# The convolution loop: a tile's matmuls are split around the next tile's last batch of transposes, and layer norm steps move behind the one-hot rows

## What is computed

```
x = x + deformable_conv(group_norm(x))        # 3 x 3 taps, learned offsets and masks
t = t + mamba_both_ways(layer_norm(t))        # two selective scans, forward and backward
t = t + graph_attention_moe(layer_norm(t))    # 262144 edges gate 4 experts
```

## Time and profile before

| what | value |
|---|---|
| median of 3 runs | 798.39 us |
| the 3 runs | 789.85, 798.39, 799.4 us |
| the profiled execution, its own time | 788.7 us |
| its span, first to last instruction | 786.7 us |
| mean granted TensorE clock | 0.816 |
| PE busy | 600.2 us |
| DVE busy | 644.9 us |
| ACT busy | 310.7 us |
| POOL busy | 353.6 us |

### The profile page before, as it was taken

How to read it: one execution, slowest core, us unless ns; L and a number is a source line. 1 busy time by engine, 2 the same in 40 slices (tenths; PEclk the granted TensorE clock), 3 DMA queues, 4 the chain that set the end, 5 groups by cost and what they waited for, 6 DMA issues and landing times.

```text
span 786.7 us, 11140 instructions
## 1 busy us (share of the span) xinstructions
PE 600.2 (76%) x4143; PEld 371.8 (47%) x4143; DVE 644.9 (82%) x1204; ACT 310.7 (39%) x360; POOL 353.6 (45%) x170
## 2 busy tenths in 40 slices
PE   3966989889889798985587887788787767729810
PEld 2235878778778697441232332333332563315410
DVE  4699096997997987979889999899999355687977
ACT  2233241221121213586677565556565113224220
POOL 4039044134324300035567566476666208787304
PEclk9956889989999958996599999899999855555555
DMA  8100000000000001000000000000000000011000
GB/s 221 44 1 0 2 1 3 8 1 2 9 1 2 1 8 40 0 1 0 1 0 0 0 0 0 1 0 0 0 0 0 1 8 8 8 6 8 3 1 27
DMA packets 17014, 8.21 MB, mean 10 GB/s; under 512 B 14471, under 2 KB 16200, under 8 KB 16712
## 3 DMA queue, kind: packets, MB, share of 16 engines
q1 hardware_dynamic: 15176, 7.01, 3.4%
q0 software_dynamic: 1792, 0.58, 1.3%
HBM read 6.33 MB, written 1.25 MB: 10 GB/s over the span
## 4 chain that ended last, share of the span: by engine, by line
DVE 40%; PE 26%; issue 20%; POOL 8%; SPq 3%; ACT 1%; DMA 1%; DVEq 1%; ACTq 0%; POOLq 0%
PE ps L548 9%; DVE ps L1273 9%; POOL arena L447 7%; DVE arena L1129 6%; DVE arena L1127 4%; PE ps L540 4%; DVE arena L1280 2%; PE ps L573 2%; DVE arena L1394 2%; PE ps L728 2%; DVE arena L1148 2%; PE ps L685 1%; PE ps L615 1%; DVE arena L1252 1%; DVE g L1396 1%
## 5 line engine op out<-in xcount | busy, mean ns | idle before, releaser
L441 POOL TENSOR_TENSOR arena<-arena 128x1024 f32<-128x1024 f32 x64 | 150.5, 2354 | 85.2 <-DVE arena L1280 33.9
L424 POOL TENSOR_TENSOR arena<-arena 128x1280 f32<-128x1280 f32 x16 | 94.6, 5924 | 159.1 <-DVE arena L1057 118.1
L1280 DVE TENSOR_TENSOR_SCAN arena<-arena,ps 128x1024 f32<-128x1024 f32 x64 | 146.3, 2287 | 10.2 <-ACT arena L915 2.0
L685 PE MATMUL ps<-arena,ident 128*128 128x512 f32 x256 | 127.1, 624 | 30.5 <-POOL arena L441 30.5
L919 ACT ACTIVATE arena<-ps 128x1024 f32<-128x1024 f32 x64 | 65.4, 1022 | 76.8 <-POOL arena L441 58.0
L447 POOL DMA_INDIRECT arena<-node_rows,src_idx x56 | 71.0, 1267 | 48.8 <-DMA node_rows<-hrow 32.0
L685 PEld LDWEIGHTS ps<-arena,ident 128*128 128x128 f32 x256 | 46.4, 196 | 93.9 <-POOL arena L441 55.3
L1273 DVE TENSOR_TENSOR ps<-arena,ps 128x1024 f32<-128x1024 f32 x64 | 77.3, 1208 | 3.4 <-PE ps L671 3.3
L915 ACT ACTIVATE arena<-arena,neg_a 128x1020 f32<-128x1020 f32 x64 | 73.2, 1144 | 9.9 <-DVE arena L1267 4.2
L835 ACT ACTIVATE arena<-ps 128x768 f32<-128x768 f32 x48 | 37.8, 809 | 96.2 <-PE ps L573 96.2
L540 PE MATMUL ps<-arena 128*128 128x64 f32 x576 | 75.1, 295 | 0.0
(11 more groups left out here) (310 smaller groups left out, 846.7 us busy)
## 6 DMA issues: line engine op xcount, KB each, us to landing
arena<-dram_edges SPq DMA_DIRECT2D x2, 1024.0 KB, 7.2
arena<-dram_x SPq DMA_DIRECT2D x2, 512.0 KB, 5.3
arena<-node_rows,src_idx POOLq DMA_INDIRECT x56
x_tok<-dram_x SPq DMA_DIRECT2D x1, 512.0 KB, 9.6
res_scratch<-x_tok SPq DMA_DIRECT2D x4, 128.0 KB, 1.9
arena<-res_scratch SPq DMA_DIRECT2D x1, 512.0 KB, 3.2
out<-arena SPq DMA_DIRECT2D x1, 352.0 KB, 2.3
arena<-dram_f_conv_w SPq DMA_DIRECT2D x1, 256.0 KB, 9.8
```

The source lines that it names most:

```text
L424: g.tensor_tensor(s_buf[i % 2][:, kk], wy[:, i, kk].unsqueeze(3).to_broadcast([P, POOL_TAPS, HEIGHT, WIDTH]), wx[:, i, kk].unsqueeze(2).to ...
L441: g.tensor_tensor(gg[e], hh[e], cs[e], ALU.mult).then_inc(s["g_ready"], 1)
L685: m = pe.matmul(ps[:, 4 + q, :], ident[:], gg[e][:, 512 * q:512 * q + 512], start=False, stop=True, skip_group_check=True)
L1280: v.tensor_tensor_scan(o, x0, x1, 0.0, ALU.mult, ALU.add).then_inc(s["scan_ready"], 1)
```

## The change

On PE the three batches of transposes of tile i are now in a helper `turn_s`, and the convolution of tile i - 1 is in two halves (`conv_part`, nine of the 18 products each). A tile reads: batch 0, batch 1, an xk part, first half, batch 2, second half, an xk part, then the histogram chunk if there is one. Tile 0 has one xk part where it had two, and from there on every part stands one place later: numbers 3 + 2i and 4 + 2i instead of 4 + 2i and 5 + 2i. ACT's copies follow: one behind its second batch, one behind its third. On DVE `ln_first` and `ln_end` stand behind the tile's one-hot rows instead of ahead of them; `ln_second` stays.

```
-            def conv_tail(i):
+            def conv_part(i, part):
                 b = i // 2
...
                 o = ps[:, 5 + i % 2, 0:C]
-                pe.matmul(o, ones_f[:], b_cv[:], start=True, stop=False)
-                for t in range(K2):
-                    for tau in range(2):
...
+                if part == 0:
+                    pe.wait_ge(s["st_ready"], 3 * i + 3)
+                    pe.wait_ge(s["xk_ready"], 4 * b + 4)
...
+                    pe.matmul(o, ones_f[:], b_cv[:], start=True, stop=False)
+                for n in range(K2 * part, K2 * part + K2):
+                    t, tau = n // 2, n % 2
+                    m = pe.matmul(o, s_t[i % 2][:, n, :], xk[b % 2][:, tau, C * t:C * t + C], start=False, stop=(n == 2 * K2 - 1))
+                if part:
+                    m.then_inc(s["conv_out"], 1)
+
+            def turn_s(i, q):
+
+                n = 3 * i + q
+                if n >= 2:
+                    pe.wait_ge(s["st_ready"], n - 1)
+                for v in range(6):
...
+                m.then_inc(s["st_psum"], 1)
...
             for i in range(NT):
                 pe.wait_ge(s["s_ready"], i + 1)
                 pe.wait_ge(s["s2_ready"], i + 1)
-                for q in range(3):
...
+                turn_s(i, 0)
+                turn_s(i, 1)
+                if 1 <= i < NT - 1:
+                    xk_part(3 + 2 * i)
+                if i:
+                    conv_part(i - 1, 0)
+                turn_s(i, 2)
+                if i:
+                    conv_part(i - 1, 1)
                 if i < NT - 2:
                     xk_part(4 + 2 * i)
-                if i:
-                    conv_tail(i - 1)
-                if i < NT - 2:
-                    xk_part(5 + 2 * i)
                 if i % 2 == 0 and 1 <= i // 2 < len(CHUNKS):
                     hist_chunk(i // 2 - 1)
-            conv_tail(NT - 1)
+            conv_part(NT - 1, 0)
+            conv_part(NT - 1, 1)
...
                     act.wait_ge(s["st_psum"], n + 1)
...
+                    if q == 1 and 1 <= i < NT - 1:
+                        xk_copy(3 + 2 * i)
                 if i < NT - 2:
                     xk_copy(4 + 2 * i)
-                    xk_copy(5 + 2 * i)
...
                 g = i // TPQ - 1
-                if g >= 0 and i % TPQ == 2:
-                    v.wait_ge(s["t1_ready"], TPQ * g + TPQ)
-                    ln_first(g)
-                elif g >= 0 and i % TPQ == 3:
+                if g >= 0 and i % TPQ == 3:
                     ln_second(g)
-                elif g >= 1 and i % TPQ == 0:
-                    ln_end(g - 1)
                 if i % 2 and 1 <= i // 2 <= ROUNDS:
                     k.wait()
                     extract(i // 2 - 1)
                 if 1 <= i <= 2 * len(CHUNKS):
                     onehots((i - 1) // 2, (i - 1) % 2)
+                if g >= 0 and i % TPQ == 2:
+                    v.wait_ge(s["t1_ready"], TPQ * g + TPQ)
+                    ln_first(g)
+                elif g >= 1 and i % TPQ == 0:
+                    ln_end(g - 1)
```

More of the change, by code:

```diff
@@ L525, in xk_part @@
                           w_cv[:].rearrange("p k n -> p (k n)")[:, 288 * hf:288 * hf + 288], start=True, stop=True).then_inc(s["xk_psum"], 1)
-            def conv_tail(i):
+            def conv_part(i, part):
                 b = i // 2
[L530 to L535, removed]
-                o = ps[:, 5 + i % 2, 0:C]
-                pe.matmul(o, ones_f[:], b_cv[:], start=True, stop=False)
-                for t in range(K2):
-                    for tau in range(2):
-                        m = pe.matmul(o, s_t[i % 2][:, 2 * t + tau, :], xk[b % 2][:, tau, C * t:C * t + C],
-                                      start=False, stop=(t == K2 - 1 and tau == 1))
-                m.then_inc(s["conv_out"], 1)
+                o = ps[:, 5 + i % 2, 0:C]
+                if part == 0:
+                    pe.wait_ge(s["st_ready"], 3 * i + 3)
+                    pe.wait_ge(s["xk_ready"], 4 * b + 4)
+                    if i >= 2:
+                        pe.wait_ge(s["t1_ready"], i - 1)
+                    else:
+                        pe.wait_ge(s["om_read"], OMQ)
+                    pe.matmul(o, ones_f[:], b_cv[:], start=True, stop=False)
[9 more added lines that the diff above has]
+                for v in range(6):
+                    t = 6 * q + v
+                    m = pe.transpose(ps[:, 2 * (n % 2) + v // 4, (v % 4) * P:(v % 4) * P + P],
+                                     s_rows[i % 2][:, t // 2, (t % 2) * P:(t % 2) * P + P], ident[:])
+                m.then_inc(s["st_psum"], 1)
             def hist_chunk(ch):
```

## The result

| | before | changed |
|---|---|---|
| median of 20 runs each | 794.96 us | 803.09 us |
| lowest and highest | 787.84 to 800.16 | 797.17 to 809.94 |
| ratio | | 1.013, 95% interval 1.010 to 1.016 |
| profiled execution, its time and span | 788.7, 786.7 us | 797.22, 795.2 us |
| mean granted TensorE clock | 0.816 | 0.798 |

What follows compares the result with a forecast made beforehand. The prediction took a ring of waits through DVE and PE to bound the kernel. Its terms, -2.2 - 1.1 + 0.65 = -2.7 us, set against the median of 798.39, gave 795.7 us, range 784 to 801.

Steps and rivals of the forecast that it cites:

- PE, third batch behind the first half: PE's third transposes batch moved behind half a convolution, covering ACT's copy: 0, bounds -0.3 and +0.2 us a tile.
- Rival A: Clock stays at 0.50 over the convolutions at tiles 8 and 12 after longer idle time: sum +6.2, 804.6 us; chance 0.14.
- may be low for what runs there: Argument against Rival A: tile 15's clock may be low for its work, having stayed low through 16 us of dense work.
- Rival B: Clock returns to 1.00 behind tile 15's transposes, at the kernel's end: sum -7.2, 791.2 us; chance 0.13.
- xk part ahead of the chunk, -0.56: PE's wait for ACT between convolution and xk part goes: 0.56 at tiles 2, 4, 8, 12, together -2.2 us.
- ln_first at tile 6: On DVE behind the rows: chunk 2 starts 1.64 earlier, but chunk 3's rows only 0.56; with tile 10, -1.1 us.
- ln_end at tile 8: On DVE behind the rows, which take 11.33 us and end 1.1 before PE is ready: 0 us.
- No third stop: POOL stops DVE's rows at tiles 8 and 12 only twice; a third stop would make the sum -0.5.
- Tile 14, +0.65: No chunk follows; tile 15's matrix, for which PE waits, comes 0.65 us later behind ln_first.
- the sign of being right: Listed observation that would confirm the forecast: tile 15's transposes starting about 2.7 us earlier.
- The sum: Whole kernel: -2.2 - 1.1 + 0.65 = -2.7 us, all of it reaching the end.
- The range: Whole kernel's time: 784 to 801 us, taking in both levels of runs and single cases of Rival A.

Runs made afterwards that it cites:

- e9: The changed kernel, unedited, profiled once more: 797.64 us.
- e1: The changed kernel with DVE's old order, so only the PE and ACT edits: 797.49 us, ratio 1.0072 of before.
- e10: The kernel before, unedited, profiled once more: 800.37 us.
- e2: The kernel before with only DVE's new order, ln_first and ln_end behind the one-hot rows: 793.06 us, ratio 0.9989.
- e3: The changed kernel with the three batches of transposes in one piece again: 796.04 us, ratio 1.0036 of before.
- e8: The changed kernel with 24 unread bf16 matmuls behind the second batch of transposes of tiles 4, 8 and 12: 793.56 us, ratio 1.0019 of before.
- e7: The changed kernel with transposes in one piece and 36 unread matmuls behind the last xk part of tiles 3, 7, 11, 14: 791.02 us, ratio 1.0025.
- e5: The kernel before with 36 unread matmuls behind the last xk part of tiles 3, 7, 11 and 14: 792.3 us, ratio 1.0013.
- e6: The kernel before with DVE's new order and 36 unread matmuls behind the last xk part of tiles 3, 7, 11, 14: 792.21 us, ratio 0.9992.
- e4: The changed kernel with 36 unread matmuls behind the last xk part of tiles 3, 7, 11 and 14: 783.9 us, ratio 0.9879 of before.
- e4b: The same kernel as e4, measured again on the chip of e5 to e7: 787.9 us, ratio 0.993 of before.
- e11: The kernel of e4 with 100 more unread matmuls behind tile 1: 788.79 us, ratio 0.9938 of before.

## Why the prediction was wrong, point by point

*The step that failed* is "PE, third batch behind the first half", put at 0 with bounds of -0.3 and +0.2 a tile. It weighed ACT's copies and what waits for the transposes, and gave the split no price through the clock. In the table the three executions with the split and no extra matmuls (changed, e9, e1) have 6 of 9 places among tiles 4, 8 and 12 at 14.9; the four with one piece (before, e10, e2, e3) have 2 of 12 at 15.0 or more. Such a place costs 14.89 - 9.31 = 5.6 us with the split, and 15.63 - 10.95 = 4.7 without. At tile 2, behind 4.5 to 11 us of idle time, the orders do not differ (three of seven at 0.50 with the split, three of seven without), and at tile 15 either order came out either way. So the split made the loss likelier at tiles 4, 8 and 12, and nowhere else as far as these executions show.

The granted clock of the single runs goes with their times. The 20 of the changed kernel lie at 797 to 801 us with a mean clock of 0.793 to 0.798, at 803 to 805 with 0.784 to 0.788, and at 807 to 810 with 0.777 to 0.782; those of the kernel before lie near 788 to 791, 793 to 796 and 798 to 800. Places at 0.50 are a part of these levels that "no row explains", the stretch behind the loop is another: the first profiled execution of the kernel before (no such place, 788.7 us) and e10 (two, 800.37) are 11.6 us of span apart, 6.7 of them up to the last chunk and 4.9 behind it.

*Rival A* named the clock, the two places and +6.2 us (measured: +8.1 between the medians), but had a chance of 0.14. That its 804.6 us lies so near the 803.09 is partly luck, since it was counted from the median of three runs, 798.39, and the median of 20 is 794.96. The rows spoke for more. The transposes of tile 8 stood at 0.50 in the earlier trace rows, so the clock fell there already, and the convolution behind them ran at 1.00 only because something in between had brought it back; the change edits just that. Rival A's own reason was the longer idle time. Alone it is not enough: the clock came back behind 4.49 us with 18 transposes (e2, tile 15), behind 4.48 with 12 and 24 matmuls (e8, tile 8), and behind 4.79 with 12 (e8, tile 15); and two places with the split stayed at 0.50 behind 3.69 (e1). That it plays no part is not shown: with the split and nothing added, all four places behind 4.46 to 4.50 us stayed at 0.50, and two of five behind 3.69 to 3.70. The objection that the clock at the end "may be low for what runs there" spoke for the rival: what runs there are float32 convolutions, and they are also what runs behind the 12 transposes now.

*Rival B* came true in the kernel before, by itself: in e10 and e2 the first convolution behind tile 15's transposes ran at full clock, and the last chunk came 23.4 us behind the start of these transposes instead of 26.3, 2.9 less.

*xk part ahead of the chunk, -0.56:* right where it can be seen alone. In the changed kernel's tile 4 the part follows the convolution without a wait. There the whole stretch shrank by 1.64 (10.95 to 9.31), more than 0.56, because the clock was back for the third batch and in part of the xk part.

*ln_first at tile 6:* right. From the end of chunk 1 to the start of chunk 2 it is 145.46 - 127.96 = 17.5 us, as forecast. The rows took 9.14 in the timeline, as forecast (9.05 in the chain of waits), matrix 7 came 0.56 later relative to the chunk (0.65), and the rows of chunk 3 started 28.51 behind chunk 1 instead of 29.27: -0.76, where -0.56 was forecast.

*ln_end at tile 8:* right, rows 11.33, not last. *No third stop:* right for this kernel, and only by the clock or the split: with the clock up and one piece it came (e7). The row that the prediction read for it was read a little wrong: 184.64 is the end of the product asked for at 176.02, which got in some 2.25 us earlier, behind the series (end 181.26) and DVE's matrix. The rule of the Trainium skill (SBUF — State Buffer, "Who interferes with whom"), that whoever issues first gets the shared pair of ports "for the whole instruction", is what the prediction took to let POOL in after one row. A third product asked for 0.36 or 0.54 us behind the end of the one before was let in (e5 at tiles 4 and 12, e6 and e7 at all three). One asked for 1.10 to 1.93 us behind it (before, e2, e3, e10, and e5 at tile 8, all in one piece), or 3.2 behind it in e4, stayed out until the series was over; so these bear out the row that the prediction took, and not its reading of the rule.

*Tile 14, +0.65:* the idle time ahead of tile 15 grew from 4.03 to 4.79, 0.76. But tile 15's transposes start 4.5 us later (278.16 against 273.64), where 2.7 earlier was the sign of being right.

*The sum* of -2.7 was not confirmed as a sum. Between the kernels with filler -4.4 was measured, but 3.1 of it is the split (e4b against e7), which the prediction had at 0; what is left is -1.3 (e7 against e5). That the total is near -2.7 is luck. The medians differ by +8.1, which is 10.8 us above the sum. Some 5 us at each of about two more places per execution would give that; the profiled executions have two and two places (changed) against none and two (before), so the number is not shown. *The range* ended at 801.0, since A was thought unlikely; with A at its price it should have ended above 804.6.

*Open:* why the clock comes back at one place and not at the next was not found; neither order, idle time nor piece settles it (tile 4 of the kernel before went both ways with the same 3.12 us and the same 18 transposes). How much of the loss needs DVE's new order as well (1.0072 without it, 1.013 with it) is open too.

## What to carry to other kernels

Where PE works behind an idle time, look at the granted clock of each stretch: where it falls and what runs just before it is back. Cutting the run of matmuls behind the idle time to fill another engine's wait can cost more than the wait, here some 5 us at a place against at most 0.3. Take more than one profiled execution of each kernel: the first of the kernel before was one of the lucky ones. Before an order is judged on a ring of engines, hold the clock up with unread matmuls in the idle time (e4 against e5): it shows what the order itself is worth, and here it was also the fastest version, 0.988 and 0.993 of before in two measurements. A faster piece on one engine moves the moment at which another engine's instruction gets in: with the clock up, the kernel before got a third stop at tile 4 and gained nothing.

## What the runs showed of the hardware

- The clock stayed at 0.50 while PE was busy: in the kernel before for all 16.0 us from 278.0 to 294.0, with two float32 convolutions; in the changed kernel for the 9 us of tile 8's convolution and six transposes. In five places at 0.50 (tiles 8 and 12 of the changed kernel, 2 and 4 of e10, 2 of e11) it was still at 0.50 as the histogram's bf16 matmuls began; at tile 8 it was back at 1.00 from 187.0, 4.1 us into them.
- A chunk's 296 histogram matmuls take 10.1 us with the clock at 0.50 for the first 3 us (tile 8 of the changed kernel, 10.10) or at 1.00 throughout (chunk 1 of the kernel before, 10.09).
- 24 bf16 matmuls of 128 x 128 behind 12 transposes, which had run at 0.50: the clock was at 1.00 from 178.8, 1.0 us into them (e8, tile 8).
- The same kernel with the same idle time and the same transposes came out either way (tile 4 of the kernel before: 10.95 in one profiled execution, 15.63 in another), some 5 us each time.
- The clock fell from 1.00 to 0.50 right behind an idle time of 2.05 us (e2, the last convolution: 7.84 us instead of 4.23).
- A POOL product asked for 0.36 or 0.54 us behind the end of the one before is let in between DVE's rows (stops of 2.0 to 2.2 us each, up to three: 13.51 against 7.10); one asked for 1.10 us behind it or later waits for the whole series (6.99 in e4, 8.62 in the earlier trace rows).
